# Moving 512 DMA issues of a mixture-of-experts stage from GpSimd's queue to SyncE's

## What is computed

```python
def _L1_ffn_ref(x, expert_sel, keys, values):
    ...
    sel = jax.nn.sigmoid(xt @ expert_sel.T)
    sel_val, sel_idx = jax.lax.top_k(sel, TOP_K)
    w = jnp.zeros((T, E), dtype=xt.dtype).at[jnp.arange(T)[:, None], sel_idx].add(sel_val)
    h = jax.nn.relu(jnp.einsum('td,edh->teh', xt, keys))
    out = jnp.einsum('teh,te,ehv->tv', h, w, values)
    return out.reshape(B, S, -1)
```

## Time and profile before

| | |
|---|---|
| median of 3 runs | 4235.07 us (4230.86 to 4239.56) |
| time of the profiled execution | 4230.09 us |
| its span, first to last instruction | 4228.4 us |
| mean granted TensorE clock | 0.878 of full speed |
| PE busy | 3572.0 us, 84% of the span |
| DVE busy | 2018.3 us, 48% |
| ACT busy | 1688.3 us, 40% |
| POOL busy | 769.5 us, 18% |
| SyncE's DMA queue (q1, hardware_dynamic) | 124.88 MB, 12.3% of the 16 engines' span |
| GpSimd's DMA queue (q0, software_dynamic) | 135.17 MB, 12.2% |

### The profile page before, as it was taken

One profiled execution on the slowest core, in us unless ns is written; L12 is line 12 of the kernel. 1 busy time (PEld: TensorE's weight loads), 2 busy tenths in 40 slices (PEclk: granted clock), 3 DMA queues, 4 the chain that ended last, 5 costly groups with the idle time before them and its releaser, 6 DMA issues.

```text
span 4228.4 us, 54399 instructions
## 1 busy us (share of the span) xinstructions
PE 3572.0 (84%) x18386; PEld 1839.6 (44%) x18386; DVE 2018.3 (48%) x2825; ACT 1688.3 (40%) x2604; POOL 769.5 (18%) x1051
## 2 busy tenths in 40 slices
PE   5898789887898878988889888898789987899867
PEld 2233553435534455344543445434454334533345
DVE  6335572355714566245652547425563345723533
ACT  1444335442363423634236342453334533355322
POOL 0000260003500044000530005200152001610035
PEclk7798899888998889979889788997899978999789
DMA  3011440214402143021420224211341113411134
GB/s 90 1 41 31 107 119 6 56 28 109 107 7 55 41 112 95 16 56 43 113 77 16 55 56 117 61 27 45 73 116 45 41 31 86 121 27 40 31 87 114
DMA packets 229742, 263.78 MB, mean 62 GB/s; under 512 B 137424, under 2 KB 139472, under 8 KB 229328
## 3 DMA queue, kind: packets, MB, share of 16 engines
q1 hardware_dynamic: 73808, 124.88, 12.3%
q0 software_dynamic: 155648, 135.17, 12.2%
HBM read 145.80 MB, written 9.44 MB: 37 GB/s over the span
## 4 chain that ended last, share of the span: by engine, by line
PE 54%; DVE 13%; DMA 12%; issue 9%; ACT 7%; POOL 3%; SPq 2%; DVEq 0%; ACTq 0%; POOLq 0%
PE ps_two L693 10%; PE ps_acc L588 10%; PE ps_acc L597 9%; DMA probs<-gates_dram 8%; DVE tops L1053 7%; DMA expert_sb<-experts_dram 4%; PE ps_one L540 4%; PE ps_one L542 3%; PE ps_one L541 3%; PE ps_two L657 3%; PE ps_one L693 3%; POOL nat L498 2%; PE ps_one L727 1%; SPq L424 1%; ACT stacks L843 1%
## 5 line engine op out<-in xcount | busy, mean ns | idle before, releaser
L1053 DVE TENSOR_REDUCE tops<-ps_two 128x2 bf16<-128x1024 f32 (+3 forms) x896 | 963.8, 1111 | 403.5 <-PE ps_two L657 237.1
L860 ACT ACTIVATE probs<-ps_two 128x1024 f32<-128x1024 f32 (+1 forms) x704 | 666.3, 963 | 411.4 <-PE ps_two L693 315.1
L657 PE MATMUL ps_two<-stacks 32*128 32x512 f32 (+3 forms) x1792 | 440.9, 519 | 245.2 <-DVE tops L1053 192.1
L486 POOL DMA_DIRECT2D expert_sb<-experts_dram x256 | 143.3, 561 | 2689.4 <-DVE rsum L1067 2555.3
L693 PE MATMUL ps_two<-stacks 97*128 97x512 f32 (+3 forms) x1408 | 540.6, 467 | 47.0 <-ACT probs L860 23.9
L588 PE MATMUL ps_acc<-probs,v_sb 128*32 128x512 f32 (+3 forms) x3584 | 474.3, 604 | 12.8 <-DVE rsum L1067 5.8
L693 PEld LDWEIGHTS ps_two<-stacks 97*128 97x128 f32 x1408 | 239.4, 200 | 539.9 <-issue 442.3
L597 PE MATMUL ps_acc<-probs,ones 128*32 128x512 f32 (+3 forms) x3584 | 460.6, 588 | 0.0
L498 POOL TENSOR_TENSOR nat<-expert_sb,nat 128x256 fp32r<-128x256 f32 x512 | 377.9, 743 | 359.1 <-ACT nat L804 272.3
L804 ACT CAST nat<-expert_sb 128x256 fp32r<-128x256 f32 x256 | 103.1, 406 | 844.5 <-DVE probs L1149 563.0
L657 PEld LDWEIGHTS ps_two<-stacks 32*128 32x128 f32 x1792 | 176.8, 206 | 532.2 <-DVE tops L1053 299.2
(11 more groups left out here) (129 smaller groups left out, 4652.3 us busy)
## 6 DMA issues: line engine op xcount, KB each, us to landing
stacks<-nat SPq DMA_DIRECT2D x792, 128.0 KB, 2.4
expert_sb<-experts_dram POOLq DMA_DIRECT2D x256, 256.0 KB, 5.3
probs<-gates_dram POOLq DMA_DIRECT2D x256, 256.0 KB, 8.8
x_in<-x_in_dram SPq DMA_DIRECT2D x9, 1024.0 KB, 4.9
out_dram<-x_res SPq DMA_DIRECT2D x16, 512.0 KB, 4.9
probs<-mats_dram SPq DMA_DIRECT2D x1, 2048.0 KB, 9.4
gates_dram<-w_turn SPq DMA_DIRECT2D x64, 16.0 KB, 1.5
sel_w<-sel_dram SPq DMA_DIRECT2D x1, 32.0 KB, 8.4
```

The lines of the kernel that those rows point to most:

```text
L657: mm = pe.matmul(acc[:, HALF * e:HALF * e + n_keys], q_st[rows, g, j, P * i:P * i + P], k_st[rows, g, j, HALF * kh:HALF * kh + n_keys], st ...
L860: done(act.activation(probs[:, n % 2, per * i:per * i + per, a:HALF], acc[:, :, a:HALF], ACT.Exp, scale=SCALE), s + (i,))
L1053: done(dve.reduce_max(tops[:, kh, 2 * pr:2 * pr + 2, i], acc[:, :, 0:cols(st, i, kh)], AX_X), s)
```

## The change

The functions `load_expert` and `load_gates` move from GpSimd's program to SyncE's, with the same sizes, the same sources, destinations, buffers and semaphores. 256 expert loads and 256 gates loads change their queue. The waits ahead of them move too. Within a step, SyncE issues the gates load first, and the expert load behind its wait for `vals_down`; GpSimd had them the other way round. Some line numbers shift: L486 and L491 become L408 and L413, L498 becomes L515, L424 becomes L448, L435 becomes L459 and L441 becomes L468. ScalarE, VectorE and TensorE keep their programs and their line numbers.

```diff
@@ SyncE's program
+                def load_expert(m):
+                    sp.dma_start(expert_sb[:, m % RING, :], experts[m % ET]).then_inc(expert_in[m % RING], 16)
+
+                def load_gates(m):
+                    hf, j = divmod(m, ET)
+                    row = w_dram[EPT * j:EPT * j + EPT, half(hf)]
+                    sp.dma_start(gate_bc[:, m % RING, :],
+                                 bass.AP(row.tensor, row.offset, [[T, EPT], [0, H], [1, HALF]])
+                                 ).then_inc(gate_in[m % RING], 16)
+
                 for s in sec.steps:
+                    if s[0] == "logits":
+
+                        hold(acc_read, "acc", 0)
+                        for m in range(RING):
+                            load_expert(m)
+                    if s[0] == "up":
+                        m = s[1] * ET + s[2]
+                        if 1 <= m and m - 1 + RING < NH * ET:
+
+                            read(("up",) + divmod(m - 1, ET))
+                            load_gates(m - 1 + RING)
+                        if m + RING < NH * ET:
+                            hold(vals_down, "up", m + 1)
+                            load_expert(m + RING)
...
                             sp.dma_start(w_dram[:, P * i:P * i + P],
                                          w_turn[E * (i % PH):E * (i % PH) + E, i // PH, :]).then_inc(gates_out, 16)
+                        hold(gates_out, "turn", sec.no["turn"][s], 16 * TT)
+                        for m in range(RING):
+                            load_gates(m)
@@ GpSimd's program
-                def load_expert(m):
-                    pool.dma_start(expert_sb[:, m % RING, :], experts[m % ET]).then_inc(expert_in[m % RING], 16)
-
-                def load_gates(m):
...
-                    if s[0] == "logits":
...
                         for m in range(2):
                             lower(m, keys_up, keys_parts, 0, keys_down)
-                        hold(gates_out, "turn", sec.no["turn"][s], 16 * TT)
-                        for m in range(RING):
-                            load_gates(m)
...
                         lower(m, vals_up, vals_parts, C, vals_down)
-                        if m + RING < NH * ET:
-
-                            hold(vals_down, "up", m + 1)
-                            load_expert(m + RING)
-                        if 1 <= m and m - 1 + RING < NH * ET:
-
-                            b, n = sec.bank(("up",) + divmod(m - 1, ET))
-                            hold(bank_read[b], b, n)
-                            load_gates(m - 1 + RING)
```

More of the change, by code:

```diff
@@ L501, in emit @@
                 for s in sec.steps:
-                    if s[0] == "logits":
-                        hold(acc_read, "acc", 0)
-                        for m in range(RING):
-                            load_expert(m)
                     if s[0] == "inputs":
```

## The result

The changed kernel takes 4595.95 us (median, 4594.14 to 4621.86) against 4236.14 us before: 360 us more, a ratio of 1.0857 with a 95% interval of 1.0816 to 1.0897.

A forecast was written before the change was run, and what follows sets the result against it. Load landings were taken to bound the kernel, no engine being full; gates loads on two fixed engines add 50.2 us a stage, so 4230.1 + 402 = 4632 us, predicted as 4630, range 4480 to 5150 us.

The forecast's parts named there:

- What bounds the kernel, and the width: Before the change: landings of gates and expert loads are 507 us of the chain; one gates load uses 2 of 16 engines.
- GpSimd's issues, counted at 0: Load issues leaving GpSimd, 1.37 us of a 4.6 us step, were expected to save nothing.
- SyncE's issues, counted at 0: Two load issues per step on SyncE, about 0.8 us, were expected to fit in the step at no cost.
- The fixed pair: SyncE's queue puts every gates load on the same two DMA engines, so 8 MB per stage pass through them; chance 0.62.
- The price of a load: A gates load on two fixed engines costs 5.45 us at 24.1 GB/s per engine; bounds 5.22 and 7.08 us.
- The sum: A stage takes 196.2 us against 146.0, +50.2 us; over eight stages +402 us, giving 4632 us.
- The cover of the chain behind the loads: Two or three gates loads queue up, keeping two engines busy; expert loads wait 7.6 us, and ScalarE's wait moves there.
- the case of 4912 us: TensorE's clock falls to 1.2 GHz, its work takes 231 us a stage, +35 us; shares chance 0.24 with slower load transfers.
- The rivals: Other outcomes: slower by more, chance 0.24; faster through rotating or wide loads, 0.12; no change, 0.02.
- Rotation, at 4120 us: SyncE's queue rotates loads over engine pairs or spreads them wider, nothing serializes, 110 us saved; chance 0.12.
- The slower rate of 18.5 GB/s per engine: Two fixed engines move gates no faster than before: 248.4 us a stage, 5050 us; shares chance 0.24 with a fallen clock.
- the signs that I named: Expected in traces: DMA share 0.13 to 0.3, gates landings of 12 us and more, 196 us stages, 6.1 us steps.

The follow-up runs named there:

- the split on GpSimd's queue: Each gates load written as two DMAs, one per expert, on GpSimd's queue, against the kernel before the change: 4054.51 us, ratio 0.9567.
- The split versions: Each gates load written as two DMAs, one per expert, with gates and expert loads on SyncE's or GpSimd's queue, four placements: 4000.61 to 4054.51 us.
- the version with a quarter more: Changed kernel plus a second narrow load of 128 of 512 columns beside each gates load, into an unread spare tile: 5056.99 us, ratio 1.1954.

## Why the prediction was right

*What bounds the kernel, and the width.* Right: a gates load runs on two engines. It was read from the share of 0.11 and the access pattern, and the two versions that change only the slowest dimension show it. What I under-read is the cost that this already had before. I took the narrow loads' rotation as a cover that made them cheap; the split on GpSimd's queue shows that 181 us were to be had there, with the small packets gone as well.

*GpSimd's issues, counted at 0.* Right for the total: the version that gives 256 of the 512 issues back to GpSimd takes 4601 us against 4596. GpSimd's busy time fell by 298 us, not 352, because its 512 subtractions took 432 us in place of 378; that cost nothing, since it waits 1128 us for ScalarE.

*SyncE's issues, counted at 0.* Right, but not for the reason I gave. I had 0.8 us a step that fit in. The instructions took 0.33 and 0.50 us where nothing was in the way, but took up to 7.2 us where gates loads were waiting ahead of them. SyncE from the head of the first stage:

```profile
496.17 9.36 SPq L413 DMA_DIRECT2D probs<-gates_dram  x4
506.73 3.86 SPq L408 DMA_DIRECT2D expert_sb<-experts_dram  x1
```

Four issues take 9.4 us there and an expert's issue behind them 3.9. It costs nothing only because the pair has work waiting just then.

*The fixed pair.* Right, and it was the choice on which the sign hung. The argument from issue times (0.40 us whatever the size) was weak support for it, and the lengths of those instructions turned out to depend on what waits ahead of them in the queue. The Trainium skill's rule (DMA: Bandwidth & Descriptors, section on why a DMA increments its semaphore by 16) is that a transfer's engines are the largest number up to 16 that divides the slowest dimension of both sides, and that hardware issue always takes the lowest-numbered ones. It holds here in all that the traces show: shares of 0.13, 0.24 and 0.62 for slowest dimensions of 2, 4 and 64, with no rotation on SyncE's queue (0.62 shows more than four engines, not all 16). That the engines are the lowest-numbered, no run here shows.

*The price of a load.* 5.45 us predicted, 5.10 measured (131,072 B at 25.7 GB/s), 2% below the lower of the bounds of 5.22 and 7.08. The choice between the store's rate and the gates loads' own was right: of the changed kernel's 144,268 packets 19,152 are under 512 B, where the kernel before had 137,424, so the small ones came with the narrow loads on GpSimd's queue.

*The sum.* 196.2 us a stage predicted, 193.9 measured; +402 us predicted, +392 in the profiled execution's span and +360 between the medians. Two terms err against each other: the loads cost 163 us instead of 174, and what is left beside them, 193.9 - 163.2 - 1.4 - 1.4 = 28 us, would be 1.0 us for each of the 28 expert loads instead of 0.68. No run shows that it all belongs to them. That the two errors nearly cancel, 11 us against 9 in a stage, is luck; the mechanism does not need it.

*The cover of the chain behind the loads.* Right: expert loads waited behind gates loads, ScalarE's wait moved there (226 to 964 us), and the pair stayed busy. The wait was longer than I had it, 9.5 us to landing instead of 7.6. TensorE's granted clock fell from 0.95 to 0.80 in the first stage and did not become the bound; the case of 4912 us did not come.

*The rivals.* Rotation, at 4120 us, is excluded by the shares. Its price stays untested, since in no run do narrow loads rotate on SyncE's queue. The split versions, where nothing serializes either, came out at 4001 to 4055 us. The slower rate of 18.5 GB/s per engine is excluded by the 51 GB/s of the pair. Of the signs that I named, the landings of gates loads can't be checked: the page gives no landing time for narrow loads on SyncE's queue.

## What to carry to other kernels

Before a DMA is moved to another queue, look at its width: take the DMA share of a window in which one such transfer is alone in flight, times 16. A narrow one can be cheap while successive ones rotate, and becomes a serial resource where they don't. A source that repeats rows should have the repeats as the slowest dimension, or be split so that it has. Here the split took 4.3% off with both kinds of load on GpSimd's queue and 13% with both on SyncE's, and once every load is wide the placements differ by 1.4% at most. And a chain that names a transfer's landing may name a bystander in a queue; move that transfer to another queue before you believe it.

## What the runs showed that I had not expected

- A DMA instruction on SyncE gets long when narrow loads wait ahead of it: 0.50 us when free, 5.7 us in the median with the gates loads on SyncE and the expert loads elsewhere. That it waits for room in a queue is my reading.
- Wide transfers were slower beside narrow ones even where these rotate: expert loads on GpSimd's queue landed in 5.3 us beside narrow gates loads and in 3.1 us beside wide ones. Width and small packets are not told apart here.
- On two engines a 512 B piece costs 28 ns and a 2 KB piece 80 ns, 18 against 26 GB/s per engine. The trace of the version with a quarter more shows the slower rate too: while the small pieces pass, the pair falls from 49 to 41 GB/s (1153 to 1154 us), and to 37 in shorter stretches.
- Subtractions on GpSimd (L498, then L515) took 743 ns in the mean before and 845 ns after, VectorE's L968 682 and 799 ns in the median, with the same work. GpSimd's are as long only in the three kernels where the expert loads stand behind gates loads of 512 columns on two engines (mean 843 to 851 ns, 736 to 755 in all others). No run here isolates why.
